# Attention over a context and a two-expert update: delta in two PSUM banks, first statistics shared by two engines, squares folded whole, transfers of 512 KB with a limit of two

## The reference, cut to what matters

```
def _layernorm(x, eps=1e-5):
    return (x - mean(x)) / sqrt(var(x) + eps)

def xattn(q, k, v):                       # k = v = ctx
    # heads: 64 rows each, N = 2048 positions
    qh = softmax(qh, axis=3)              # over the 64 rows of a head
    kh = softmax(kh, axis=1)              # over the 2048 positions
    kvs = einsum('bnhd,bnhe->bhde', kh, vh)
    return einsum('bnhd,bhde->bnhe', qh, kvs)

def ffn(x):
    logits = x @ router_w.T               # 4 experts, the best 2 are kept
    gates = softmax(top2(logits))
    mid = einsum('tf,erf->ter', x, A)
    return einsum('te,teo->to', gates, einsum('ter,eor->teo', mid, B) * 4.0)

x = x + xattn(_layernorm(x), ctx, ctx)
x = x + ffn(_layernorm(x))
```

## Time and profile before

| | us |
|---|---|
| median of 3 runs (489.4 to 492.21) | 490.92 |
| the profiled execution | 484.94 |
| its span, first to last instruction | 483.1 |

### The profile page before, as it was taken

One profiled execution on the slowest core, in us unless ns is written; L12 is line 12 of the kernel. 1 busy time (PEld: TensorE's weight loads), 2 busy tenths in 40 slices (PEclk: granted clock), 3 DMA queues, 4 the chain that ended last, 5 costly groups with the idle time before them and its releaser, 6 DMA issues.

```text
span 483.1 us, 22236 instructions
## 1 busy us (share of the span) xinstructions
PE 395.0 (82%) x9448; PEld 338.9 (70%) x9448; DVE 379.2 (78%) x1013; ACT 360.2 (75%) x468; POOL 378.4 (78%) x341
## 2 busy tenths in 40 slices
PE   5378877798988797988979789798899889989664
PEld 4367766687877686877768678677688677877543
DVE  2258678899998886987979889797979889778652
ACT  2469998889888885977888879797868789774200
POOL 0467999799999896987989898997979799976300
PEclk9558899899999997988999999999979999999955
DMA  8998888589998999979798989989797979554336
GB/s 279 398 388 262 254 276 273 187 270 361 277 383 254 368 297 303 305 242 372 230 370 300 358 293 303 380 270 381 265 324 236 360 288 312 181 187 153 118 137 224
DMA packets 75282, 137.95 MB, mean 286 GB/s; under 512 B 8240, under 2 KB 10416, under 8 KB 75056
## 3 DMA queue, kind: packets, MB, share of 16 engines
q1 hardware_dynamic: 75184, 136.54, 83.2%
HBM read 102.95 MB, written 33.55 MB: 283 GB/s over the span
## 4 chain that ended last, share of the span: by engine, by line
PE 46%; DVE 17%; issue 13%; POOL 12%; SPq 5%; DMA 4%; ACT 2%; DVEq 0%; POOLq 0%; ACTq 0%
PE num_ps L396 11%; PE kv_ps L377 10%; PE delta_ps L459 9%; PE raw_ps L413 8%; POOL y_sb L316 6%; POOL ek_sb L304 5%; PE delta_ps L460 5%; DVE y_sb L683 5%; DVE max_n L611 2%; DMA ctx_sb<-in_ctxt_dram 2%; DVE sq_b L652 2%; PE kv_ps L426 2%; DVE attnT L674 2%; SPq L231 2%; SPq L226 2%
## 5 line engine op out<-in xcount | busy, mean ns | idle before, releaser
L316 POOL TENSOR_TENSOR y_sb<-attnT,y_sb 128x512 f32<-128x512 f32 x128 | 172.8, 1351 | 41.1 <-DVE attnT L674 26.5
L304 POOL TENSOR_TENSOR ek_sb<-ctx_sb,kmax_row 128x512 f32<-128x512 f32 x128 | 172.1, 1346 | 28.5 <-ACT kmax_row L492 28.5
L683 DVE TENSOR_TENSOR y_sb<-delta_ps,y_sb 128x512 f32<-128x512 f32 x128 | 87.8, 686 | 35.3 <-PE delta_ps L460 33.9
L396 PE MATMUL num_ps<-kv_sb,x_sb 64*64 64x65 f32 x4096 | 96.8, 230 | 17.5 <-issue 10.5
L377 PE MATMUL kv_ps<-ctx_sb,ek_sb 128*64 128x65 f32 x2048 | 96.7, 237 | 12.1 <-issue 9.3
L396 PEld LDWEIGHTS num_ps<-kv_sb,x_sb 64*64 64x64 f32 x4096 | 77.7, 139 | 35.4 <-issue 25.5
L413 PE MATMUL raw_ps<-w_sb,y_sb 128*64 128x69 f32 x2048 | 90.6, 228 | 12.0 <-issue 12.0
L611 DVE TENSOR_REDUCE max_n<-ctx_sb 128x32 f32<-128x512 f32 x128 | 86.2, 677 | 15.4 <-DMA ctx_sb<-in_ctxt_dram 15.4
L459 PE MATMUL delta_ps<-midT,b_hi 128*128 128x256 f32 x256 | 84.8, 351 | 15.6 <-DVE y_sb L683 15.2
L377 PEld LDWEIGHTS kv_ps<-ctx_sb,ek_sb 128*64 128x64 f32 x2048 | 77.0, 143 | 22.9 <-issue 10.8
L674 DVE TENSOR_TENSOR attnT<-num_ps,rden 128x512 f32<-128x512 f32 x128 | 88.5, 692 | 4.4
(11 more groups left out here) (57 smaller groups left out, 345.9 us busy)
## 6 DMA issues: line engine op xcount, KB each, us to landing
ctx_sb<-in_ctxt_dram SPq DMA_DIRECT2D x128, 260.0 KB, 6.0
x_sb<-in_x_dram SPq DMA_DIRECT2D x128, 256.0 KB, 6.0
y_sb<-in_xt_dram SPq DMA_DIRECT2D x128, 256.0 KB, 5.9
out_dram<-y_sb SPq DMA_DIRECT2D x128, 256.0 KB, 5.6
sq_a<-in_bt_dram SPq DMA_DIRECT2D x1, 1024.0 KB, 11.4
w_sb<-in_wt_dram SPq DMA_DIRECT2D x1, 552.0 KB, 7.4
cst<-in_consts_dram SPq DMA_DIRECT2D x1, 145.0 KB, 2.2
```

The source lines that it names most:

```text
L304: pool.tensor_tensor(ek_sb[:, t % 2, chunks(g), :].rearrange("p (a b) c -> p a b c", b=2), ctx_sb[:, t % 4, 2 * g:2 * g + 2, 1:P + 1, :].r ...
L316: pool.tensor_tensor(y, attnT[:, g, :], y, ALU.add).then_inc(x1_made, 1)
L396: mm = pe.matmul(num_ps[n, h, j * (DH + 1):(j + 1) * (DH + 1)], x_sb[d, t % 4, c * P + half * DH:c * P + (half + 1) * DH], kv_sb[d, t % 2, ...
L683: dve.tensor_tensor(y, delta_ps[:].rearrange("p (j t c) -> p t j c", j=2, t=2), y, ALU.add).then_inc(out_made, 1)
```

## The change

- **Delta.** `delta_ps` becomes two banks used in turn; `delta(p, i)` waits for the addition of piece i - 2. The bank of `turn_ps` is given up: the turned maximum goes to unused columns of the numerator's bank, the spread maximum to unused columns of the bank of keys x values. The spreading transpose moves behind the numerator in TensorE's step, ScalarE's copy of the row moves behind the exponential of the second half of the keys, and VectorE's whole maximum moves behind the delta's addition. New waits keep the shared banks safe.
- **Statistics.** For even tiles VectorE makes mean and variance of x by `bn_stats` on each quarter and `bn_aggr`; ScalarE sums and squares the odd tiles only.
- **Squares.** `halve_squares` is gone; TensorE folds both halves, 32 passes in place of 16.
- **Transfers.** PIECES = 2: halves of 512 KB, and SyncE's loop goes in steps of two. In an iteration come the store, x, xt and ctx, in this order, and each also waits until the transfer two before it has landed. x is issued 10 steps ahead in place of 11. The last pair's eight stores and the transfers ahead of the loop have no such limit.

```diff
-            PIECES = 4
+            PIECES = 2
...
-            for q in range(0, 4 * NT + 28):
+            STEP = 4 // PIECES
+            ctx_piece = x_piece = xt_piece = out_piece = (cst_landed, 16)
+            for q in range(0, 4 * NT + 28, STEP):
+                last = q + STEP - 1
                 p, r = divmod(q - 26, 8)
                 if 0 <= p < NP - 1:
-                    after(sp, delta_done, quarters_done(q, 21))
-                    sp.wait_ge(out_made, 8 * p + 2 * (r // 2) + 2)
-                    store(2 * p + r % 2, r // 2)
-                t, r = divmod(q + 11, 4)
+                    t, k = 2 * p + r // STEP % 2, r // (2 * STEP)
+                    after(sp, raw_done, quarters_done(q - 1, 7))
+                    sp.wait_ge(out_made, 8 * p + 8 // PIECES * (k + 1))
+                    after(sp, *xt_piece)
+                    store(t, k)
+                    out_piece = (out_stored[t % 8], 32 * (t // 8) + 16 * (k + 1))
+                t, r = divmod(q + 10, 4)
                 if 3 <= t < NT:
-                    after(sp, num_done, 4 * (t - 4) + r + 1)
-                    load_x(t, r)
-                t, r = divmod(q + 16, 4)
-                if t < NT:
-                    sp.wait_ge(kv_done, 4 * (t - 4) + r + 1)
-                    load_ctx(t, r)
+                    after(sp, num_done, 4 * (t - 4) + r + STEP)
+                    after(sp, *ctx_piece)
+                    load_x(t, r // STEP)
+                    x_piece = (x_landed[t % 4], 32 * (t // 4) + 16 * (r // STEP + 1))
                 t, r = divmod(q, 4)
                 if 2 <= t < NT:
                     after(sp, raw_done, quarters_done(q, 7))
                     if t >= 8:
                         sp.wait_ge(out_stored[t % 8], 16 * PIECES * (t // 8))
-                    load_y(t, r)
+                    after(sp, *out_piece)
+                    load_y(t, r // STEP)
+                    xt_piece = (y_landed[t % 8], 32 * (t // 8) + 16 * (r // STEP + 1))
+                t, r = divmod(q + 16, 4)
+                if t < NT:
+                    sp.wait_ge(kv_done, 4 * (t - 4) + r + STEP)
+                    after(sp, *x_piece)
+                    load_ctx(t, r // STEP)
+                    ctx_piece = (ctx_landed[t % 4], 32 * (t // 4) + 16 * (r // STEP + 1))
...
             def spread_kmax(q):
                 pe.wait_ge(kmax_made, t + 1)
-                pe.transpose(turn_ps[:, P:2 * P], kmax[:, t % 2:t % 2 + 1].to_broadcast([P, P]),
+                after(pe, kv_copied, t - 1)
+                pe.transpose(kv_ps[t % 2][:, P:2 * P], kmax[:, t % 2:t % 2 + 1].to_broadcast([P, P]),
...
             def fold_squares(q):
-                pe.wait_ge(sq_halved, t + 1)
+                pe.wait_ge(sq_made, 2 * t + 2)
                 after(pe, kv_copied, min(t + 2, NT))
-                for k in range(2):
+                after(pe, row_made, min(t + 4, NT))
+                for k in range(NCH // 4):
                     for s in range(4):
...
             def delta(p, i):
-                after(pe, out_made, 8 * p + i)
+                after(pe, out_made, 8 * p + i - 1)
...
-                    to = delta_ps[:, k * 2 * P:(k + 1) * 2 * P]
+                    to = delta_ps[i % 2][:, k * 2 * P:(k + 1) * 2 * P]
...
                 delta(*delta_at(q))
                 turn_max(q)
-                spread_kmax(q)
                 sum_squares(q)
...
                 numerator(*tile_at(q, 5))
+                spread_kmax(q)
                 kv(*tile_at(q, 0))
...
             def sum_x(t):
-                if not 0 <= t < NT:
+                if not 0 <= t < NT or t % 2 == 0:
                     return
...
+            def bn_part(t, g):
+                if t is None or t % 2:
+                    return
+                if g == 0:
+                    dve.wait_ge(x_landed[t % 4], 32 * (t // 4 + 1))
+                dve.bn_stats(bn_parts[:, t % 4, g, :], x_sb[:, t % 4, cols(g)]).then_inc(bn_parts_made, 1)
...
-            def halve_squares(q):
-                dve.wait_ge(sq_made, 2 * t + 2)
-                dve.tensor_tensor(sq_b[:], sq_b[:], sq_a[:, t % 2, :], ALU.add).then_inc(sq_halved, 1)
...
                 if r == 1:
+                    keys(T, 1)
                     spread_row(T + 1)
-                    keys(T, 1)
...
                 max_part(*tile_at(q, -8))
-                halve_squares(q)
                 kv_recip(q)
...
-                if not early:
-                    max_whole(q)
                 mid_low(q)
+                bn_part(*tile_at(q, -5))
                 add_delta(*delta_at(q))
...
+                if not early:
+                    max_whole(q)
                 normalise(*tile_at(q, 5))
```

More of the change, by code:

```diff
@@ L81, in xattn_lora_moe_kernel @@
         rz = sb("rz", [P, 2])
+        bn_parts = sb("bn_parts", [P, 4, G, 6])
+        bn_out = sb("bn_out", [P, 4, 2])
         x_sum = sb("x_sum", [P, 4])
@@ L118, in xattn_lora_moe_kernel @@
         num_ps = bank("num_ps", (P, 2, 512))
-        delta_ps = bank("delta_ps")
-        turn_ps = bank("turn_ps")
+        delta_ps = [bank("delta_ps0"), bank("delta_ps1")]
+        max_ps = num_ps[:, 0, 3 * P:4 * P]
         ctx_landed = [sem(f"ctx_landed{i}") for i in range(4)]
@@ L158, in xattn_lora_moe_kernel @@
         kmax_made = sem("kmax_made")
+        bn_parts_made = sem("bn_parts_made")
+        bn_made = sem("bn_made")
         negmean1_made = sem("negmean1_made")
@@ L353, in turn_max @@
                 pe.wait_ge(max_made, 4 * t + 4)
-                after(pe, row_made, t)
-                pe.transpose(turn_ps[:, 0:P], max_n[:, t % 2, :], ident).then_inc(maxT_done, 1)
+                after(pe, attn_made, 4 * (t - 3) + 3)
+                pe.transpose(max_ps, max_n[:, t % 2, :], ident).then_inc(maxT_done, 1)
             def spread_kmax(q):
@@ L386, in numerator @@
                     pe.wait_ge(kv_copied, t + 1)
+                    pe.wait_ge(kmax_made, min(t + 3, NT))
                 if g % 2 == 0:
@@ L491, in spread_row @@
                 after(act, shifted, 4 * (t - 1))
-                act.activation(kmax_row[:, t % 2, :], turn_ps[:, P:2 * P], ACT.Copy).then_inc(row_made, 1)
+                act.activation(kmax_row[:, t % 2, :], kv_ps[t % 2][:, P:2 * P], ACT.Copy).then_inc(row_made, 1)
             def sum_x(t):
-                if not 0 <= t < NT:
+                if not 0 <= t < NT or t % 2 == 0:
                     return
-                act.wait_ge(x_landed[t % 4], 64 * (t // 4 + 1))
-                after(act, x_squared, t)
+                act.wait_ge(x_landed[t % 4], 32 * (t // 4 + 1))
+                after(act, x_squared, t // 2)
                 act.activation(junk[:], x_sb[:, t % 4, :], ACT.Copy,
@@ L502, in square_x @@
             def square_x(t):
-                if not 0 <= t < NT:
+                if not 0 <= t < NT or t % 2 == 0:
                     return
-                act.wait_ge(negmean1_made, t + 1)
+                act.wait_ge(negmean1_made, t // 2 + 1)
                 act.activation(junk[:], x_sb[:, t % 4, :], ACT.Square, bias=negmean1[:, t % 4:t % 4 + 1],
@@ L633, in ln1_var @@
                     return
-                dve.wait_ge(x_squared, t + 1)
-                dve.tensor_scalar(var1e[:, t % 4:t % 4 + 1], x_sq[:, t % 4:t % 4 + 1], 1.0 / N, EPS, ALU.mult,
-                                  ALU.add).then_inc(var1e_made, 1)
+                i = t % 4
+                if t % 2:
+                    dve.wait_ge(x_squared, t // 2 + 1)
+                    dve.tensor_scalar(var1e[:, i:i + 1], x_sq[:, i:i + 1], 1.0 / N, EPS, ALU.mult,
+                                      ALU.add).then_inc(var1e_made, 1)
+                else:
+                    dve.wait_ge(bn_parts_made, 2 * t + 4)
+                    dve.bn_aggr(bn_out[:, i, :], bn_parts[:, i, :, :].rearrange("p g s -> p (g s)")).then_inc(bn_made, 1)
+                    dve.wait_ge(bn_made, t // 2 + 1)
+                    dve.tensor_scalar(var1e[:, i:i + 1], bn_out[:, i, 1:2], EPS, None, ALU.add).then_inc(var1e_made, 1)
             def ln1_bias(q):
```

30 lines of the change are left out of this document (16 added, 14 removed).

## The result

The changed kernel takes a median 600.0 us (598.5 to 601.7, 4 runs) against 490.16 us (487.2 to 492.21, 4 runs): a ratio of 1.234, 95% interval 1.227 to 1.241. The forecast was 510 us, slower, with a range up to 543 us: the direction holds, the size doesn't, by a factor of five and a half (110 us in place of 20). A ratio and its interval leave out executions over 1.5% above the fastest of the same kernel; a median is taken over all of them.

What follows compares the result with a forecast made beforehand. A chain of ctx and x loads, two transfers in flight, was to bound the kernel: 428.2 + 81.3 - 7 = 502.5 us of span, + 1.8 = 504.3, + 6.0 = 510 us; range 465 to 543 us.

Steps and rivals of the forecast that it cites:

- chain ctx - x - ctx: SyncE's loop: ctx and x loads wait for each other, 110 links of 3.57 us, last ctx half at 428.2 us.
- L: Time from issue to landing of a 512 KB load with two in flight: taken as 3.5 us, ends 2.9 and 4.7.
- sum: Span of the whole kernel: 428.2 us of chain + 81.3 to the end - 7 for delta = 502.5 us.
- rival D: SyncE's loads stay slow with so little under way: L = 4.0 us, 565 us in all; chance 0.13.
- second chain: SyncE's loop: store and xt wait for each other, one transfer of them under way; named without a price.
- 6.0 us added for the median: Whole kernel: the median of three runs, 490.92 us, lay 6.0 us above the profiled execution; added at the end.
- Transfers: SyncE's loop: halves, two in flight, make a step 3.57 us where today's pace is 3.35 us.
- Delta: Last additions: PE no longer waits for the addition before, 7 us gained at the end, bounds 5 and 12.
- Statistics: ACT loses 68 us; DVE's 64 new instructions at 0.68 us offset the dropped halving, bounds -22 to +43 us.
- Squares: PE's fold of 32 passes: 21.7 us more busy time, hidden under the chain, up to 22 us without it.
- Row: ACT's row of the keys' maximum comes 0.9 us later: 16 us of POOL idle, 0 to 43, hidden under the chain.
- Rival B: Large transfers land as fast as small ones, SyncE's stalls end: 478 us, middle 470; chance 0.30 together with a never-binding throttle.

Runs made afterwards that it cites:

- after_no_limit: The changed kernel with its halves, order and gates, but without the wait for the transfer two before: 495.9 us, ratio 1.019 to the kernel before.
- rest_alone: The changed kernel with SyncE's loop of the kernel before (quarters, no limit), all other parts of the change kept: 486.3 us, ratio 1.003.
- delta_banks_only: The kernel before with only delta in two banks and the new places and waits of the turned maxima: 479.1 us, ratio 0.976.
- transfers_alone: The kernel before with SyncE's loop of the changed kernel (halves, two in flight), all compute as before: 617.0 us, ratio 1.274.
- light_transfers: The kernel before, each ctx, xt and output transfer from tile 8 on moving a quarter of its bytes: 461.0 us, ratio 0.948.

## Why the prediction was wrong

**The mechanism was right.** The forecast named the chain ctx - x - ctx of single transfers as the new limit, with 110 links to the last half of ctx. The trace has it: 60% of the ending chain are loads of x and ctx and 10% loads of xt and stores, SP waits for landings, the engines for x and xt. That each 0.1 us of L costs 11 us held too; the break-even near L = 3.3 us was not tested.

**The mis-sized term is L: taken as 3.5 us, it was 4.29 us**, the mean landing in the chain (4.36 a link less 0.07; those 0.07 us held, though the rows they were read from give 0.11 with a rounded landing). 110 x 0.79 = 87 us of the 95.6 us by which the span (598.1 us) exceeds the 502.5 us of the sum. Two choices went into the 3.5. The mean of 3.3 us for lone loads of 256 KB was sound (3.0 us by themselves). The step that failed is the other, that the second 256 KB costs only some 0.2 us, as half of a load's time passes before bytes flow and the rest overlaps the other chain. Before bytes flow passes 0.96 us, a third of the 3.0 us of 256 KB and a quarter of the 3.8 us of 512 KB, and the second 256 KB costs 0.8 us alone, which the prediction had between its ends as 0.7 us. The two chains also lengthen each other, which had no term: two loads of x in flight take 4.4 us and not 3.8, and in the kernel's order, where one of the two is often a store, a link takes 4.0 us. That makes some 0.3 us for the bytes, 0.2 us for the other chain and 0.3 us that was there only with the engines at work. The upper end, 4.7 us, was in the text, but the range stopped at 3.8 us: it gave rival D, 565 us at L = 4.0 us, 0.13 and left it outside. D was the right case in kind and fell short in size. It argued with the 187 GB/s of the shallow stretch and was priced at the 367 GB/s of the deep one; with 187 GB/s, L = 4.7 us, its own sum gives 642 us, so that the 600 us lie between its two rates.

**The rest of the difference.** The chain reached its end 4.7 us earlier than its links alone say (its first transfer went out at 26.3 us, not 29.6, and its last landed 4.5 us after issue; the sum has 5.9 us for the first: 3.3 + 1.4). From the last ctx landing (505.7 + 4.5 = 510.2 us) to the end passed 87.9 us and not 74.3: step 116 began at 516.2 us, 6.0 us after the landing, and from there it took 81.9 us as before (81.3 us), not 7 less. The gain of the two banks is there in the additions. But the sum has this stretch as compute alone, and the second chain, which the prediction named and gave no price, runs through it: the ending chain goes through xt and stores up to 567.9 us, the last half of xt going out at 564.0 us. 86.7 - 4.7 + 13.6 = 95.6 us. The 6.0 us added for the median were wrong here: the profiled execution took 599.9 us, the median is 600.0.

**Step by step.** *Transfers:* right in kind, mis-sized. *Delta:* the size held, 7 us predicted, 7.5 by the medians and 11.5 by the ratio, and it is the one part that pays; but partly by luck: the additions came closer than 1.2 us, and some of that was lost to the stores. (By the rows the wait that goes is 2.01 - 1.18 = 0.83 us a piece, and not 0.75.) *Statistics:* right: 0.688 us an instruction for 0.68, 0.25 us for the combination, VectorE's total 380.6 us for 379.2. *Squares:* 40.9 us for 21.7, +19.2 as predicted with +21.7; without effect, as predicted under the chain, and even without the limit, which the prediction had left open (up to 22 us). *Row:* late, as said, though the 0.9 us it was to be late had no working; 54.3 us of GpSimd's waits in the kernel after, which there stand beside the chain; about 1% or nothing without the limit. *Rival B's account* (L small, 478 us in the middle case) is what after_no_limit and rest_alone test: 496 and 486 us. It failed in the middle: the waits of GpSimd for xt and half of those for VectorE do not turn into time.

**What stays open.** rest_alone gives nothing though its end is 8.6 us shorter, because the stretch ahead of the end is 11.8 us longer. Which part does that is not settled: undoing the row gives about 1% or nothing, undoing the fold nothing; the shared statistics were not undone by themselves (delta_banks_only, which undoes all three, is 2.6 points ahead of rest_alone by the ratios, 0.6 by the medians). Open is also why a link is 0.3 us longer with the engines at work.

## What to carry to other kernels

A limit on transfers in flight is a limit on bytes per landing time: measure the landing of a transfer of that size with that many beside it, in a kernel of nothing but transfers, before relying on small pieces' landings, and expect more beside the engines (here 4.03 us became 4.29). If a queue's landing times look long, ask whether they are the depth that carries the rate; here 5.9 us at 1.85 MB in flight was healthy, 4.3 us at 1.05 MB was not. If two chains of waits come of a limit, price both, to the end of the kernel. And a change of many parts hides its good one: delta in two PSUM banks was worth 1.5 to 2.4%.

## What the runs showed of the hardware

**Rate by bytes in flight, loads of x by themselves:** 1.05 MB in flight moved at 243 GB/s as two of 512 KB, 2.1 MB at 397 GB/s as four. The bytes in flight aren't all, the number of pieces counts too: 1.05 MB moved at 219 GB/s as one of 1 MB and at 264 GB/s as four of 256 KB, and 2.1 MB at 330 GB/s as two of 1 MB, each by its bytes over the time between issues in the rows shown above.

**TensorE stops in the middle of a row of equal matmuls.** In the kernel before, the timeline around 205 us shows one (start, duration, and in brackets the idle time before):

```profile
204.07 0.47 PE L377 MATMUL kv_ps<-ctx_sb,ek_sb 128*64 128x65 f32 x8
...
206.57 0.46 PE L377 MATMUL kv_ps<-ctx_sb,ek_sb 128*64 128x65 f32 x8 [2.04 <-issue]
```

Nothing is waited for between the eighth and the ninth of these matmuls, and TensorE stands for 2.04 us. Between 100 and 400 us there are 24 such stops (the next matmul of the row starts over half a microsecond late), 35 us. The trace also has 16 KB packets of instructions on a queue of their own (q8, 74 in the kernel before), on the same DMA engines; all 24 stops end 1.2 to 1.6 us after such a packet has ended (the expectation above had 1.1 to 1.3). With a limit of two there is 1 stop (1.3 us) in the kernel after and none in transfers_alone; with three 10 (17 us), with four 23 (37 us). So under the limit of two the stops are gone; that this buys time isn't shown, as TensorE is then idle anyway. Four quarters in flight have 6 stops (5 us). That such a packet ends shortly before every stop's end points to instructions that came late; no run changes the packets alone. Whether a shorter queue or a slower TensorE is what ends the stops is open: in the limited kernels both hold, and in light_transfers, where TensorE is quick, it is the load that is lower.
